# The DMA that puts a unit's row of maxima into the stack, issued from SyncE's queue instead of ScalarE's

## The reference

```python
# layer 0, one attention (the cross one has no mask)
att = jnp.einsum('bhqd,bhkd->bhqk', q, k) * scale
att = jnp.where(causal[None, None], att, -jnp.inf)
y = jnp.einsum('bhqk,bhkd->bhqd', jax.nn.softmax(att, axis=-1), v)
...
x = x + xattn0(layernorm(x), ctx)     # self + cross, one output projection
x = x + ffn0(layernorm(x))            # bitlinear, exact gelu, bitlinear
x = x + xattn1(layernorm(x), ctx)
x = x + ffn1(layernorm(x))            # per-tensor 8 bit, exact gelu
```

## Time and profile before

| what | us |
|---|---|
| median of three runs | 1818.75 (1816.89 to 1820.31) |
| the profiled execution, its own time | 1820.03 |
| its span | 1818.2 |
| PE busy | 1619.8 (89%) |
| DVE busy | 1386.8 (76%) |
| ACT busy | 1149.8 (63%) |
| POOL busy | 654.4 (36%) |

### The profile page before, as it was taken

How to read it: one execution, slowest core, us unless ns; L and a number is a source line. 1 busy time by engine, 2 the same in 40 slices (tenths; PEclk the granted TensorE clock), 3 DMA queues, 4 the chain that set the end, 5 groups by cost and what they waited for, 6 DMA issues and landing times.

```text
span 1818.2 us, 28822 instructions
## 1 busy us (share of the span) xinstructions
PE 1619.8 (89%) x9552; PEld 704.9 (39%) x9552; DVE 1386.8 (76%) x3221; ACT 1149.8 (63%) x2182; POOL 654.4 (36%) x914
## 2 busy tenths in 40 slices
PE   5998889998999989998999999988999998899677
PEld 1343334423443434433443344423443443333226
DVE  5778868778687787778787778878588787687287
ACT  1474475666765685667665685657655855765497
POOL 2436223551454133631454135522562242310140
PEclk7899889999999999999999999999999998999898
DMA  7444313323242323342242323332332231133113
GB/s 188 135 117 120 79 36 100 88 71 99 54 113 76 94 60 100 88 110 61 71 117 63 85 77 93 87 103 74 85 106 60 54 100 50 45 87 130 48 70 117
DMA packets 106948, 159.46 MB, mean 88 GB/s; under 512 B 20656, under 2 KB 83248, under 8 KB 106800
## 3 DMA queue, kind: packets, MB, share of 16 engines
q1 hardware_dynamic: 101208, 155.25, 30.6%
q10 hardware_dynamic: 5592, 2.36, 0.6%
HBM read 105.00 MB, written 51.38 MB: 86 GB/s over the span
## 4 chain that ended last, share of the span: by engine, by line
PE 55%; DVE 19%; ACT 12%; POOL 6%; issue 5%; DMA 1%; ACTq 1%; SPq 0%; DVEq 0%; POOLq 0%
PE acc L1564 12%; PE st L1550 11%; PE misc L1531 10%; PE misc L1507 7%; DVE nmax L1330 7%; PE misc L1479 4%; ACT probs L1046 3%; PE misc L1591 3%; PE misc L1519 3%; ACT tail_h L1116 2%; DVE misc L1324 2%; ACT hq L1075 1%; ACT tail_h L1101 1%; PE misc L1618 1%; PE misc L1605 1%
## 5 line engine op out<-in xcount | busy, mean ns | idle before, releaser
L1046 ACT ACTIVATE probs<-st 128x512 f32<-128x512 f32 (+3 forms) x1536 | 758.3, 552 | 370.8 <-PE st L1550 232.9
L1330 DVE TENSOR_REDUCE nmax<-misc 128x1 f32<-128x512 f32 x1024 | 650.6, 682 | 170.1 <-PE misc L1531 168.7
L1531 PE MATMUL misc<-stack 96*128 96x512 bf16 (+3 forms) x1536 | 526.4, 366 | 74.5 <-DVE nmax L1330 47.3
L1550 PE MATMUL st<-stack 99*128 99x512 bf16 (+3 forms) x1536 | 543.9, 365 | 38.2 <-ACT probs L1046 35.4
L1324 DVE CUSTOM_DVE_ANT_0 misc<-misc,mask_mx 128x384 f32<-128x384 f32 (+3 forms) x512 | 239.5, 516 | 97.3 <-PE misc L1531 93.0
L1550 PEld LDWEIGHTS st<-stack 99*128 99x128 bf16 x1536 | 149.1, 99 | 379.4 <-ACT probs L1046 233.3
L1531 PEld LDWEIGHTS misc<-stack 96*128 96x128 bf16 x1536 | 148.2, 100 | 227.0 <-DVE nmax L1330 87.8
L1564 PE MATMUL acc<-probs,v_x 128*32 128x512 f32 x1152 | 160.3, 630 | 0.0
L904 POOL TENSOR_TENSOR parts<-qk,zero 128x512 bf16<-128x512 f32 x77 | 80.0, 1039 | 220.8 <-ACT qk L1011 220.8
L1564 PE MATMUL acc<-probs,v_s 128*32 128x512 f32 (+3 forms) x1152 | 117.0, 479 | 0.1
L1553 PE MATMUL st<-mask_st,identb 128*128 128x128 bf16 x512 | 112.1, 222 | 0.0
(11 more groups left out here) (269 smaller groups left out, 2097.8 us busy)
## 6 DMA issues: line engine op xcount, KB each, us to landing
parts_xk<-parts SPq DMA_DIRECT2D x54, 128.0 KB
stack<-parts_xk SPq DMA_DIRECT2D x36, 192.0 KB, 3.6
parts_xq<-parts SPq DMA_DIRECT2D x51, 128.0 KB
stack<-parts_xq SPq DMA_DIRECT2D x34, 192.0 KB, 3.1
parts_sk<-parts SPq DMA_DIRECT2D x48, 128.0 KB
parts_sq<-parts SPq DMA_DIRECT2D x48, 128.0 KB
stack<-parts_sq SPq DMA_DIRECT2D x32, 192.0 KB, 2.8
stack<-parts_sk SPq DMA_DIRECT2D x32, 192.0 KB, 3.4
```

The source lines that it names most:

```text
L1046: act.activation(probs[:, j % P_SLOTS, c, T - w:], st_bank(n, 4 * j + c)[:, 0:w], ACT.Exp, scale=SCALE).then_inc(exp_done, 1)
L1330: dve.tensor_reduce(nmax[:, ring, first:first + NT * (len(cs) - 1) + 1:NT], src, AX.X, ALU.max, negate=True).then_inc(misc_free[slot], 1)
L1531: last = pe.matmul(o, stack[0:ROWS, r, 0, c, P * i:P * i + P], stack[0:ROWS, r, 1, c, 0:w], start=True, stop=True)
L1550: last = pe.matmul(o[:, 0:w], stack[0:AUG, r, 1, c, P * j:P * j + P], stack[0:AUG, r, 0, c, T - w:T], start=True, stop=not causal)
```

## The change

SP gets a function for the step `negmax_T`: it waits until ACT has copied the row into `nrow` and issues the same DMA with the same semaphore. ACT keeps the copy and loses its wait for it and the issue.

```diff
@@ SP @@
+            def negmax_T(s):
+                r = s.n.slot(2)
+                wait_misc_read(sp, s)
+                sp.dma_start(stack[ROWS:AUG, s.n.slot(STACKS), 0, :, :].rearrange("o c (i t) -> o (c i) t", i=NT),
+                             nrow[:, r, :]).then_inc(negmax_landed[r], 16)
...
-            walk(sp, dict(..., project=project, settle=settle,
+            walk(sp, dict(..., project=project, settle=settle, negmax_T=negmax_T,
...
@@ ACT @@
             def negmax_T(s):
                 r = s.n.slot(2)
                 act.wait_ge(negmax_landed[r], s.n.round(2).times(16, 16).at())
                 copy_misc(s, 0, nrow[:, r, :], lambda b: as_bf16(b)[0:PARTS * HU * NT, 0:P])
-                wait_misc_read(act, s)
-                act.dma_start(stack[ROWS:AUG, s.n.slot(STACKS), 0, :, :].rearrange("o c (i t) -> o (c i) t", i=NT),
-                              nrow[:, r, :]).then_inc(negmax_landed[r], 16)
```

More of the change, by code:

```diff
@@ L774, in finish_most @@
                     finish(s)
-            walk(sp, dict(consts_load=consts_load, w_load=w_load, weights=weights, load0=load0, load1=load1, load_mid=load_mid, project=project, settle=settle,
+            walk(sp, dict(consts_load=consts_load, w_load=w_load, weights=weights, load0=load0, load1=load1, load_mid=load_mid, project=project, settle=settle, negmax_T=negmax_T,
                           stack=stack_, finish=finish_most))
```

## The result

The kernel with the row issued by SP takes 1858.4 us (median of four runs, 1852.01 to 1862.56), the kernel before 1817.82 us (four runs, 1814.9 to 1820.31). The ratio is 1.0217 with a 95% interval of 1.0201 to 1.0234: 40.6 us slower. The profiled execution took 1862.56 us, 1860.8 of it span, at a mean granted clock of 0.946 (before: 0.952).

The account below looks back on a forecast made before the run. The kernel was taken as mostly an instruction stream on PE in fixed order. Five turns at net 4.3 us (21.5) plus about +1 outside gave +23 us on 1818.75: 1842 us, own range 1827 to 1864, 8 in 10 within 1817 to 1872.

Parts of the forecast that it names:

- the five turns: Pattern repeating five times, 201 us apart: each loses 6.0 us, gains 1.7, net 4.3; 21.5 us in all.
- What SP gets: SP gets a wait for ACT's copy and 96 issues of 0.73 us; late rows stall PE in s1, s2, s3, f2, x0.
- The assumed landing of 2.6 us: Time from SP's issue of the row to its landing, taken near the low end, behind three writes of 128 KB.
- The rule of the Trainium skill: All engines' DMAs share 16 DMA engines, so the move costs nothing and saves ACT's issue time; faster rival, 1796 at most, chance 0.11.
- s1 and s2, 0.2 + 0.4 predicted: Units s1 and s2 of a turn: PE late by 1.7 and 0.9 us, of which 0.2 and 0.4 are counted.
- x0, for which 1.4 was predicted: Unit x0 of a turn, row behind the write parts_sq: PE late by 1.7 us, 1.4 counted.
- the cover of 0.3: In x0 PE idles 1.3 of 27.6 us; 0.3 of that was taken to absorb part of the stall.
- s3, 2.3 predicted: Unit s3 of a turn, row behind the write parts_xk: PE has no gap, so 2.3 us is paid in full.
- f2, 1.7 predicted: Unit f2 of a turn, row behind the write parts_sk: DVE shifts along with PE, so 1.7 us is paid.
- ACT's gain, 1.7 a turn predicted: Where ACT sets the pace, 634.7 to 667.5, two rows of 0.83 us drop off ACT: 1.7 us gained a turn.
- Outside the turns, 7.5 - 5 - 1.25 predicted: First batch and late turns: nine late units sum to 15 us, half counted; less ACT's 5 and the tail's 1.25, about +1.
- The gain of the tail: Last unit but one: PE's 1.25 us wait for a row caught behind SP's large loads for the tail goes away.

Follow-up runs that it names:

- experiment 5: Kernel after, but the row goes out after SP's wait for the split and ahead of the three writes: 1819.38 us, ratio to before 1.0014.
- experiment 3: Kernel before, with SP also waiting for ACT's copy and sending a spare DMA of the same size at the row's place: 1816.23 us, ratio 0.9996.
- 1: Kernel after, with the row issued by SP ahead of the SP step that stood just before it: 1800.69 us, ratio to before 0.9905.
- 2: Kernel after, but SP issues the row only in 48 units where nothing stands ahead of it, ACT in the other 48: 1810.6 us, ratio to before 0.9954.
- Experiment 9: Kernel after, with the row put ahead of the preceding SP step only in s1, s2 and x0 of the five turns: 1840.32 us, ratio to before 1.0127.
- Experiment 7: Kernel after, with the row put ahead of the preceding SP step only in s3 of the five turns: 1849.71 us, ratio to before 1.0171.
- Experiment 8: Kernel after, with the row put ahead of the preceding SP step only in f2 of the five turns: 1852.9 us, ratio to before 1.0223.
- experiment 4: Kernel after, with ACT's wait for its copy and an issue put back as a spare DMA: 1862.17 us, ratio to before 1.0238.
- 6: Kernel after, with the row ahead of the preceding SP step and ACT's wait and issue put back as a spare DMA: 1810.67 us, ratio to before 0.9964.
- experiment 10: Kernel after, with the row put ahead of the preceding SP step everywhere but in s1, s2, s3, f2 and x0 of the five turns: 1838.09 us, ratio 1.0123.

## Why the prediction came out as it did

The direction, the mechanism and the places were right; the forecast of +23 us was 18 short of the measured 40.6. By the traces the five turns grew by 28.4 us, where 21.5 were forecast, and all the rest by 14.1, where 1 was. So more of the miss lies outside the turns, and inside them large errors partly cancelled, which is luck.

**What SP gets.** The profile shows what the prediction asked for: 96 issues on SP, 24 waits of PE in five turns, at s1, s2, s3, f2 and x0. The assumed landing of 2.6 us was right: behind the three writes the row lands 2.60 to 2.65 us after its issue in the second turn. With no write just ahead of it, as in experiment 5, it takes 2.2 us.

**The rule of the Trainium skill** (DMA: Bandwidth & Descriptors, section Issuing engines are not separate DMA queues) came out half right. The transfer itself cares little who issues it: experiment 3 shows the extra issues at no cost, and in 1 and 2 the move saves time. But what an issuing engine also lends is its program order, and by that the same 96 DMAs cost 2.2% or save 1.0%.

**s1 and s2, 0.2 + 0.4 predicted.** This step failed. In the trace the two cost 4.5 us in the first turn and 0.7 to 2.3 in the others, 10.3 in five. From the second turn on s1 came out as predicted: PE waits 1.6 us for its row, and by the time that PE wants the row of s2, all but 0.2 us of that or less has been made good (in the third turn PE is even 0.6 us early). But s2 then waits as well, 0.5 to 2.2 us, because its row stands behind `load_mid`. In the second turn:

```profile
526.70 1.55 SPq L733 DMA_DIRECT2D xmid<-in_x_dram  x1
528.29 0.77 SPq L770 DMA_DIRECT2D stack<-nrow  x1
```

```profile
531.93 0.39 PE L1553 MATMUL st<-stack 99*128 99x512 bf16 x1 [1.69 <-DMA stack<-nrow]
```

Behind this load of 512 KB the row lands 3.6 to 4.7 us after its issue, and 2.6 was assumed. And the first turn is not like the others, though the prediction took one pattern for all five. Already before, SP was done with the write ahead of s1 at 297.98 there, when PE had wanted the row at 296.35; the prediction's own subtraction gives 4.2 us late, not 1.7. SP before, and PE after:

```profile
295.84 2.14 SPq L747 DMA_DIRECT2D parts_fk<-parts  x3
```

```profile
310.13 0.61 PE L1553 MATMUL st<-stack 99*128 99x512 bf16 x1 [4.12 <-DMA stack<-nrow]
```

With x0, for which 1.4 was predicted and the trace shows 1.7 to 1.8 (the cover of 0.3 was not there), this makes 19 us in five turns. Experiment 9 gives back 18.1, where the prediction's terms say 10.

**s3, 2.3 predicted.** This held. PE waits 2.3 to 2.4 us in every turn, and the stretch from s2 to s3 grows by that much or more. Experiment 7 gives back 8.7 us, 1.7 a turn; its interval, 3 to 14, does not exclude the full 12.

**f2, 1.7 predicted.** This step failed the other way. PE does wait 1.6 to 2.0 us, but the stretch from f2 to f3 is then shorter by 2.7 to 2.8 us in all five turns. These are the windows of the second turn before and after (columns as in the earlier trace rows):

```profile
573.20:592.90 19.70, 16.50 (x75) 4.71 (x74) 15.01 (x29) 10.57 (x20) 9.96 (x13) 0.91 0.23 69
```

```profile
596.50:613.40 16.90, 14.69 (x73) 4.52 (x73) 13.82 (x29) 9.91 (x19) 7.61 (x11) 1.00 0.26 71
```

PE, DVE and ACT do the same work in less busy time. Experiment 8, which has f2 in time again, shows that only part of this comes from the late row. The same stretch there, also of the second turn:

```profile
591.08:609.14 18.06, 16.04 (x74) 4.55 (x73) 14.98 (x29) 10.59 (x20) 9.43 (x12) 0.91 0.27 75
```

DVE is as busy as before, about 15.0 us where it is 13.8 after, but the stretch takes 18.1 us in four of the five turns, not 19.7. So the late row shortens the stretch by 1.1 us, and f2 costs the rest of its wait, 0.5 to 0.8 us a turn, not 1.7. The other 1.6 us of a turn, 8 in five, are a fall of the clock that before has at one place in all five turns and that was missing there, with the row late (after) or in time (experiment 8); the prediction had no term for it. It hid 8 us of the loss, of which falls of the clock elsewhere in the turns took back some 6.5: s3 to f0 took 15.7 us in the first turn and 17.1 in the fifth, where it takes 14.0 in the others, and the fifth turn's s2 to s3 took 18.2, not 16.6. Experiment 8 itself, whose median is 5.5 us below that of the kernel after, is too noisy to show either. The last section looks at both parts.

**ACT's gain, 1.7 a turn predicted.** In the kernel after at most 0.8 a turn is seen (experiment 4: some 4 us in all); a late PE leaves ACT time to issue. Where the rows are in time the gain is there: 10 us between experiments 6 and 1.

**Outside the turns, 7.5 - 5 - 1.25 predicted.** This step failed too, and by most. The half that was to be absorbed was not: PE's waits there, 18.4 us, are a little above the sum of 15 that the prediction began from, and experiment 10, which removes most of them, gives back 20.3 us (12 to 22), where 7.5 was counted. Its trace runs 7 us ahead of before in these stretches; that would fit the gains predicted there (6.25), but the traced run of experiment 3, which takes as long as before, is 3.6 us ahead there as well, so traces tell this only roughly. The gain of the tail came as predicted: the last unit but one no longer waits.

So the error lies mainly in three places: the slack credited outside the turns was not there, s2 was taken to land like a row behind a write, and the first turn was taken to be like the second. The missing fall of the clock in f2 hid part of that, most of which the falls elsewhere took back. Experiments 7, 9 and 10 add up to 47 us, with 8 (5.5, not told from nothing) to 53; all rows together give 58 in experiment 1. The difference is within the intervals of the four.

**Left open.** Of the 17.6 us that experiment 1 gains over before, 10 are ACT's. Of the other 7.6, the row that was caught behind the tail's loads is 1.25, and the clock may be some 2 or 3 (last section). The rest was not separated.

## What to carry to other kernels

Moving a DMA to another engine's queue moves it into that engine's program order. Before such a move, look not at how busy the queue is but at what the instruction ahead waits for, add its issue time and the landing, and subtract that from the time at which the consumer wants the data; then place the DMA ahead of the step that stands. Take the landing behind what really stands ahead: here 2.6 us behind three writes and 3.6 to 4.7 behind one large load. Do the subtraction for every turn, not for one. Count a stall on the path in full unless the trace shows the same slack at that very place: s1 had it, the stretches outside the turns did not. And where a transfer is late by a microsecond or two, even the issues just ahead of it decide.

## What the runs showed of the hardware

**Small DVE operations beside POOL.** In f2 before, POOL's split runs while DVE does a few operations on 128x4 numbers. POOL first, then DVE, in the second turn:

```profile
576.50 1.04 POOL L908 TENSOR_TENSOR parts<-qk,zero 128x512 bf16<-128x512 f32 x1
577.62 1.16 POOL L910 TENSOR_TENSOR parts<-qk,parts 128x512 bf16<-128x512 f32 x1
```

```profile
576.94 0.62 DVE L1241 TENSOR_TENSOR tok_xam<-tok_xmax,tok_xr 128x4 f32<-128x4 f32 x1
...
577.90 0.91 DVE L1246 TENSOR_SCALAR tok_xs<-tok_xam,wscale 128x4 f32<-128x4 f32 x1
```

Two of them take 0.62 and 0.91 us and end at 577.56 and 578.81, within 0.03 us of the end of POOL's operation beside them (577.54 and 578.78). In the kernel after, f2 is late, POOL's split ends at 600.29, and the same two come at its end and behind it:

```profile
599.13 1.16 POOL L916 TENSOR_TENSOR parts<-qk,parts 128x512 bf16<-128x512 f32 x1
```

```profile
600.26 0.22 DVE L1244 TENSOR_TENSOR tok_xam<-tok_xmax,tok_xr 128x4 f32<-128x4 f32 x1
...
600.81 0.20 DVE L1249 TENSOR_SCALAR tok_xs<-tok_xam,wscale 128x4 f32<-128x4 f32 x1
```

They take 0.22 and 0.20 us: 1.1 us of the 2.8. In experiment 8, where f2 is in time again, they are back at 0.62 and 0.91. The Trainium skill (SBUF — State Buffer, section SBUF: two separate sides) says that a GpSimd operation and a DVE operation that has two inputs in SBUF, or runs in a two-port mode, need the same pair of ports, and that the one that starts first holds it for its whole instruction. These three traces agree with that; no run took POOL's work away to show it by itself.

**The clock of PE.** The other part of the shorter f2 is a fall of the clock that came at this place before and not after. The four projection matmuls behind the same wait, before, after and in experiment 8:

```profile
585.05 3.03 PE L1507 MATMUL misc<-xnT_A,W 128*128 128x512 f32 x4 [0.20 <-DVE nmax L1330]
```

```profile
607.25 1.98 PE L1510 MATMUL misc<-xnT_A,W 128*128 128x512 f32 x4 [0.21 <-DVE nmax L1333]
```

```profile
602.95 1.98 PE L1532 MATMUL misc<-xnT_A,W 128*128 128x512 f32 x4 [0.21 <-DVE nmax L1355]
```

Before, the granted clock was 0.51 from 585.8 to 589.2 us, so close to the lower level (1.2 GHz); after, it was 1.00 over the whole stretch (2.4 GHz). In experiment 8 the mean over the stretch is 0.91, as before, but the clock had fallen sooner, from 598.3 to 601.7, and was back when these matmuls ran. In the third turn of the kernel after, too, it was 0.90 from 801.7 to 818.6, and the stretch still took 16.9 us. So what a fall costs depends on where it comes.

In another turn it cost more: at 1147.32 PE had just waited 2.22 us for the row of s2, and about a microsecond later the clock fell for 3.4 us. The window:

```profile
1148.40:1151.80 3.40, 3.40 (x11) 2.63 (x10) 1.84 (x4) 0.66 (x2) 0.00 (x0) 0.56 0.30 65
```

The stretch from s2 to s3 took 18.2 us in this turn, where it takes 16.6 in the others with the same wait for s3. That the wait brought the fall is not shown: in the third turn PE waited 1.66 us at the same place, and no fall followed. So a wait of PE can cost more than its length, or less. Over the whole run the clock is a small part of the result: the fastest run after (1852.01 us) had a mean clock of 0.955, and the eight runs of before at 0.955 to 0.957 took 1813.75 to 1817.85 us (median 1815.5), a difference of some 37 us at the same clock, against 40.6 between the medians. In the same way the three runs of experiment 1 at 0.954 and 0.955 (1799.02 to 1805.12 us) lie some 15 us below the three of before at 0.954 on the same chip (1813.47 to 1816.8), not 17.6.
